# Around the attention stage of a two-layer model: where the low part of the inverse matrix is made, an early use of Gelu, the first block rows of the experts, and the place of the result rows

## The chip, the cores and the metric

One core of a Trainium2 chip runs the whole program in one launch. The metric is the device time in microseconds (us) of that core. TensorE multiplies (PE in the rows, its weight loads are PEld), VectorE is DVE, ScalarE is ACT, GpSimd is POOL, and SyncE (SP) only starts transfers. A queue of SP, ACT or POOL is written SPq, ACTq, POOLq.

## What is computed

Two layers on x of 8 x 512 x 256 (the batch b has 8 entries), all in float32. Cut to what matters here:

```python
xn = layernorm(x)
x = x + attention(xn) * silu(ffn(xn))          # layer 0: causal attention, 16 heads of 16
xn = layernorm(x)
# layer 1, s: a long convolution. v = short 3-tap filter of one branch of a projection,
# conv = irfft(rfft(v) * rfft(filter)), s = (branch * conv) @ out_w + out_b
# layer 1, g: mixture of 20 experts, 2 for each row
h = gelu(xn @ wg1 + bg1); probs = softmax(h @ wg2 + bg2); top 2 of 20
y[row] = sum over its 2 experts of prob * (xn[row] @ We[e] + be[e])
x = x + s * silu(y)
```

## The kernel before, in words

The program is three blocks of code (`with nc.Block()`), each with one instruction stream for each engine. A block ends when all five engines have come to its end; GpSimd's stream ends with a drain. The order of work within a stream is written out by hand, and semaphores join the streams.

**Block 1 (from L641).** For each b: attention and feed-forward of layer 0, the residual, the norm of layer 1 (`norm(b, NORM_X1)`, whose rows are made by L1365), the transposed normed rows `xn2T`, the router (hidden layer with Gelu L1195, logits, softmax with Exp L1199, top 2, ranks L616 to L629) and `send` (L637): eight indirect DMAs of GpSimd, which scatter the rows to `slots_in`, sorted by expert. The routing of b runs during the attention of b+1; for the last b, 7, it stands alone behind the attention. There the streams also prepare layer 1's convolution: the inverse transform's matrix `Inv` is split into a high part (ACT, L1320) and a low part (POOL, L1771, which reads the staging tile `st_i`), and the first projection, short filter and forward transform are run. GpSimd's stream there is: low part of `Win` (L1767), the power that gives 1/std of the norm (`power`, L1683), low part of `Inv` (L1771), a wait for the ranks, a tiny operation (L1774), eight sends. VectorE's is: norm of b = 7, `short_filter(0)`, `split_x1(7)`, router, ranks, `split_v_low(0)`, `block_tables()`. The last of these makes `block_row` and `block_expert` (L1633, L1634): for each of 84 blocks of 128 rows, where it starts in `slots_in` and which expert it has.

**Block 2 (from L1835), the expert stage.** 84 blocks, 6 in a ring (14 turns of 6). SP reads the block's row out of SBUF into a register (`value_load`, L1822) and starts the transfer of 128 rows (L1824) into one of 12 places of `xb`. TensorE transposes them (L1856), ACT copies (L1893), TensorE multiplies by the expert's matrix (L1871), DVE adds the bias (L1915), ACT stores three blocks at a time (L1901). TensorE waits for three blocks' transfers at a time (semaphore `xb_in`, one for each half of a ring). DVE also does the product with the filter of the convolution's entry b = 0 in seven parts (`with_filter`, first at the second turn) and writes it to `Z`, which lies over `st_win` and `st_i`. GpSimd has nothing in this block.

**Block 3 (from L1976), the last stage.** Turn b = 0 to 7. TensorE's turn is `pe_turn`: projection of b+1, `back_whole(b)` (the inverse transform's first half, needs the first split of `Z`), `transposes(b+1)` (L347), `back_mixed(b)` (L371), `forward(b+1)` (L302, waits for `v2_lo`, the low part of the filtered branch), `project_out(b)` (L383). ACT follows with copies out of PSUM; `transformed` (L417) gives `Vf`, the transform that DVE multiplies by the filter. DVE's turn for b = 1 to 6 is: `filtered(b)` (first instruction L469, which waits for two of the four `Vf`), `branch_out(b-1)`, `short_filter(b+1)` (L440), `split_z_low(b, 1)` (L453), `split_v_low(b+1)` (L447, waits for ACT's L409 and makes `v2_lo`), `gated(b)` (L526, waits for L371), `result_rows(b-1)` (L1969 and L1973: product with the gate, sum with the residual rows), `second_choice(b)` (L1961, four instructions). GpSimd gathers the experts' rows (L2050) for ACT's `first_choice` and DVE's `second_choice`.

Of the kernel before, what the change touches and what calls it, by code (L numbers as in the profile page):

```python
# [11 lines left out]
ALU = mybir.AluOpType  # L12
# [3 lines left out]
P = 128  # L16
# [17 lines left out]
NROWS = NE * CAP  # L34
# [20 lines left out]
def program(nc, x, wqkvT, woutT, wguT, wdT, wg1, bg1, wg2, bg2, winT, bin_, short, wo2, bo2, fw1, fb1, fw2, fb2,  # L55
# [15 lines left out]
    with ctx:  # L71
# [103 lines left out]
        rinv = keep("rinv", [P, NT, NH])  # L175
        idle_p = keep("idle_p", [P, NH])
        idle_v = keep("idle_v", [P, 2])
        Mneg = keep("Mneg", [P, 1, NT, GH])
        Mhi = keep("Mhi", [P, NT, GH], F32R)
        Mparts = keep("Mparts", [P, 2, GH, NT])  # L180
# [275 lines left out]
        def with_filter(dve, b, part):  # L456

            def step(ins):
                ins.then_inc(U["dstep"], 1)

            def done(n):
                dve.wait_ge(U["dstep"], ND * b + n)

            flat = lambda ap: ap.rearrange("p q c -> p (q c)")
            re = lambda h_: flat(Vf[:, h_, 0:2, :])
            im = lambda h_: flat(Vf[:, h_, 2:4, :])
            tb = lambda t_, h_: flat(t_[:, h_, :, :])
            def mul(at, a_, b_):
                step(dve.tensor_tensor(at, a_, b_, ALU.mult))  # L469

            t = [tmp[:, n, :] for n in range(4)]
            q = [tmq[:, n, :] for n in range(4)]
            if part == 0:
                dve.wait_ge(U["vf_sb"], 4 * b + 2)
                at_least(dve, U["z_lo"], 2 * b)
                mul(t[0], re(0), tb(HA, 0))
                mul(t[1], im(0), tb(HB, 0))
                mul(t[2], re(0), tb(HB, 0))
            if part == 1:
                mul(t[3], im(0), tb(HN, 0))  # L480
                done(2)
                step(dve.tensor_tensor(flat(Z[:, 0, 0:2, :]), t[0], t[1], ALU.subtract))
                done(4)
                step(dve.tensor_tensor(flat(Z[:, 0, 2:4, :]), t[2], t[3], ALU.add))
            if part == 2:
                mul(q[0], re(0), tb(HA, 1))
                mul(q[1], im(0), tb(HB, 1))
                mul(q[2], re(0), tb(HB, 1))
            if part == 3:
                mul(q[3], im(0), tb(HN, 1))  # L490
                dve.wait_ge(U["vf_sb"], 4 * b + 4)
                done(6)
                mul(t[0], re(1), tb(HA, 0))
                mul(t[1], im(1), tb(HB, 0))
            if part == 4:
                mul(t[2], re(1), tb(HB, 0))
                mul(t[3], im(1), tb(HN, 0))
                done(10)
                step(dve.tensor_tensor(q[0], q[0], q[1], ALU.subtract))
            if part == 5:  # L500
                step(dve.tensor_tensor(q[2], q[2], q[3], ALU.add))  # L501
                done(14)
                step(dve.tensor_tensor(t[0], t[0], t[1], ALU.subtract))  # L503
                step(dve.tensor_tensor(t[2], t[2], t[3], ALU.add))  # L504
            if part == 6:
                done(17)
                at_least(dve, U["s_ps"], 2 * b)
                step(dve.tensor_tensor(flat(Z[:, 1, 0:2, :]), q[0], t[0], ALU.add))
                done(18)
                step(dve.tensor_tensor(flat(Z[:, 1, 2:4, :]), q[2], t[2], ALU.add))  # L510
# [130 lines left out]
        with nc.Block() as block:  # L641
# [493 lines left out]
            def _(act):  # L1135
# [184 lines left out]
                act.activation(Inv[:, HI, :, :], st_i[:, :, :], ACT.Copy).then_inc(t_hi, 1)  # L1320
                projected(act, 0, (0, 1))
                first_tap(act, 0)
                split_x1(B - 1)
                projected(act, 0, (2,))
                route_hidden(B - 1)
# [354 lines left out]
            def _(pool):  # L1680
# [86 lines left out]
                pool.tensor_tensor(Win[:, LO, :, :], st_win[:, :, :], f(Win[:, HI, :, :]), ALU.subtract  # L1767
                                   ).then_inc(t_lo, 1)
                power(B - 1, veps2, rstd2, "ln2_var", "ln2_std")
                pool.wait_ge(t_hi, 3)  # L1770
                pool.tensor_tensor(Inv[:, LO, :, :], st_i[:, :, :], f(Inv[:, HI, :, :]), ALU.subtract)  # L1771
                pool.wait_ge(S["ranked"], B)
                pool.wait_ge(S["ln2_done"], NT * B)
                pool.tensor_tensor(idle_v[:, 1:2], neghalf[:, 0:1], neghalf[:, 0:1], ALU.mult)  # L1774
# [43 lines left out]

            return ap.rearrange("(j k p) d -> j p k d", p=P, k=HALF)[n]

        def load_block(sp, block, after=0):
            row = sp.value_load(block_row[0:1, block:block + 1], min_val=0, max_val=NROWS - P)  # L1822
            at_least(sp, transposed, after)
            sp.dma_start(xb[:, block % AHEAD, :], slots_in[bass.ds(row, P), :]  # L1824
                         ).then_inc(xb_in[block % AHEAD // HALF], 16)
# [9 lines left out]
        with nc.Block() as block:  # L1835
            @block.sync
            def _(sp):
                sp.wait_ge(S["sent"], 128 * B)
                for n in range(NBLK):
                    load_block(sp, n, after=n - AHEAD + 1)  # L1840
                    if n == AHEAD:
                        sp.dma_start(bo2b[:, :], bo2.partition_broadcast(P)).then_inc(U["wo_in"], 16)
                sp.wait_ge(U["wo_in"], 32)
# [44 lines left out]
            def _(act):  # L1888
# [12 lines left out]
                    act.dma_start(half_rows(slots_out, h_), yb[:, HALF * (h_ % 2):HALF * (h_ % 2) + HALF, :]  # L1901
                                  ).then_inc(yb_out[h_ % 2], 16)

                in_turns(act, lambda: None, turn)
                store(NBLK - 1)

            @block.vector
            def _(dve):
# [67 lines left out]
        with nc.Block() as block:  # L1976
# [39 lines left out]
            def _(dve):  # L2016
                for b in range(B):
# [6 lines left out]
                    if not last:  # L2024
                        short_filter(dve, b + 1)
                        split_z_low(dve, b, 1)
                        split_v_low(dve, b + 1)
                        gated(dve, b)
                    else:
                        split_z_low(dve, b, 1)  # L2030
                    if b > 0:
                        result_rows(dve, b - 1)
                    second_choice(dve, b)
                    if last:
# [75 lines left out]
```

## Time and profile before

| what | value |
| --- | --- |
| device time, median of 3 runs | 1112.41 us (1111.92 to 1112.5) |
| the profiled execution, device time | 1105.52 us |
| its span | 1103.8 us |
| busy share over the span: PE, DVE, ACT, POOL | 89%, 65%, 44%, 37% |

The page of the profile cuts the span into 40 equal slices of 27.6 us. Each digit is the busy share in tenths (9 is 90% or more); PEclk is the granted clock of TensorE in tenths.

```profile
PE   1889999999999999999999999966599989999995
PEld 1765776676686686686586676645366768888884
DVE  7556465576676666666667456546266338999997
ACT  2434544544635635534545543453122334444441
POOL 6203312522522532441441452263000044778860
PEclk9978997998998998998999996997899999999998
DMA  4863944542642733634534540087467743334421
```

Slices 1 to 26 are block 1; slices 27 to 29 hold the work behind the last attention, the change of blocks and the start of the expert stage; the expert stage ends in slice 33, and the last stage fills the rest. The share of a busy engine is a mean over stages: what a change is worth is read from the rows of its stage.

### The profile page before, as it was taken

The numbers are of one execution on the slowest core, as the hardware profiler recorded it, in microseconds if no ns is written. First come the engines' busy times: TensorE is split into PE (matmuls) and PEld (weight loads), VectorE is DVE, ScalarE is ACT, GpSimd is POOL, SyncE is SP. The second block draws the span as 40 slices with busy tenths as digits, with TensorE's granted clock in tenths as the row PEclk, the third lists the DMA queues.
The fourth block names the chain that finished last, engine by engine and source line by source line (L and its number), as shares of the span: only waits on it lengthen the run. The fifth ranks groups of instructions, "written<-read, shape, count | busy, mean of one in ns | idle before, by whom it ended". The sixth has DMA issues, their size and how long they took to land. (4 is left out here: it accounts for less than half of the span.)

```text
span 1103.8 us, 19164 instructions
## 1 busy us (share of the span) xinstructions
PE 978.5 (89%) x5936; PEld 746.5 (68%) x5936; DVE 717.7 (65%) x1459; ACT 480.2 (44%) x887; POOL 408.9 (37%) x610
## 2 busy tenths in 40 slices
PE   1889999999999999999999999966599989999995
PEld 1765776676686686686586676645366768888884
DVE  7556465576676666666667456546266338999997
ACT  2434544544635635534545543453122334444441
POOL 6203312522522532441441452263000044778860
PEclk9978997998998998998999996997899999999998
DMA  4863944542642733634534540087467743334421
GB/s 172 160 149 61 172 155 60 108 162 44 113 148 53 116 131 81 90 123 115 77 97 135 82 125 29 2 288 274 129 202 215 217 174 100 110 123 131 131 80 38
DMA packets 87596, 137.23 MB, mean 124 GB/s; under 512 B 9907, under 2 KB 63347, under 8 KB 85364
## 3 DMA queue, kind: packets, MB, share of 16 engines
q1 hardware_dynamic: 69188, 101.40, 37.5%
q0 software_dynamic: 6144, 16.79, 4.9%
q10 hardware_dynamic: 12208, 18.35, 4.7%
q8 instruction: 28, 0.46, 0.2%
q14 instruction: 28, 0.23, 0.1%
HBM read 79.88 MB, written 55.57 MB: 123 GB/s over the span
## 5 line engine op out<-in xcount | busy, mean ns | idle before, releaser
L1449 DVE TENSOR_REDUCE Mneg<-PS 128x2 f32<-128x1024 f32 (+2 forms) x192 | 195.6, 1043 | 103.8 <-PE PS L961 103.6
L1210 ACT ACTIVATE PT<-PS 128x512 f32<-128x512 f32 (+1 forms) x384 | 170.0, 537 | 165.6 <-PE PS L985 165.2
L1698 POOL TENSOR_TENSOR idle_p<-neghalf 128x1 f32<-128x1 f32 x128 | 25.1, 196 | 353.7 <-ACT PT L1210 353.7
L985 PE MATMUL PS<-qs,ks 96*128 96x512 f32 (+3 forms) x512 | 140.8, 388 | 12.2 <-ACT PT L1210 5.7
L957 PE MATMUL PS<-ks,qs 96*128 96x256 f32 (+3 forms) x512 | 132.8, 371 | 0.8 <-DVE Mneg L1449 0.8
L985 PEld LDWEIGHTS PS<-qs,ks 96*128 96x128 f32 x512 | 96.9, 210 | 42.1 <-ACT PT L1210 25.7
L785 PE MATMUL PS<-xnT,Wgu 128*128 128x512 f32 x384 | 104.5, 414 | 4.0 <-ACT V L1155 2.4
L1871 PE MATMUL PS<-Wes,xbT 128*128 x336 | 97.3, 397 | 3.8 <-issue 2.1
L1704 POOL TENSOR_SCALAR_AFFINE_SELECT PT<-PT 128x256 f32<-128x256 f32 x256 | 99.7, 413 | 0.0
L957 PEld LDWEIGHTS PS<-ks,qs 96*128 96x128 f32 x512 | 86.8, 218 | 11.1 <-issue 7.6
L785 PEld LDWEIGHTS PS<-xnT,Wgu 128*128 128x128 f32 x384 | 71.0, 194 | 23.5 <-DVE h L1392 2.9
L998 PE MATMUL PS<-PT,V 128*32 128x512 f32 (+3 forms) x1024 | 82.1, 464 | 4.1 <-POOL PT L1704 4.0
L1687 POOL TENSOR_TENSOR h<-h,h 128x512 fp32r<-128x512 f32 x40 | 51.3, 1288 | 65.7 <-ACT h L1174 65.6
L1915 DVE TENSOR_TENSOR yb<-PS,bes 128x256 f32<-128x256 f32 x84 | 35.2, 424 | 62.1 <-PE PS L1871 53.0
L2046 POOL TENSOR_TENSOR idle_q<-ident 128x1 f32<-128x1 f32 x8 | 66.6, 8319 | 23.6 <-DVE acc L1961 23.6
L2050 POOL DMA_INDIRECT yg<-slots_out,pos x64 | 66.7, 1043 | 18.6 <-issue 17.6
L961 PE MATMUL PS<-mask,ident 128*128 128x128 f16 (+2 forms) x352 | 69.6, 276 | 0.0
L1871 PEld LDWEIGHTS PS<-Wes,xbT 128*128 128x128 f32 x336 | 52.3, 191 | 24.5 <-issue 22.1
L637 POOL DMA_INDIRECT slots_in<-xn,rows_now x64 | 62.3, 974 | 17.5 <-issue 17.5
L1893 ACT ACTIVATE xbT<-PS 128x256 f32<-128x256 f32 x84 | 31.6, 384 | 85.1 <-PE PS L1856 64.2
L998 PEld LDWEIGHTS PS<-PT,V 128*32 128x32 f32 x1024 | 32.2, 116 | 51.0 <-issue 40.5
L1392 DVE SCALAR_TENSOR_TENSOR h<-PS,sil 128x512 f32<-128x512 f32 x48 | 32.5, 689 | 44.4 <-ACT sil L1167 31.7
(227 smaller groups left out, 1760.3 us busy)
## 6 DMA issues: line engine op xcount, KB each, us to landing
qs<-qk_parts SPq DMA_DIRECT2D x96, 128.0 KB
ks<-qk_parts SPq DMA_DIRECT2D x96, 128.0 KB
xb<-slots_in SPq DMA_DIRECT2D x84, 128.0 KB, 2.3
slots_out<-yb ACTq DMA_DIRECT2D x28, 384.0 KB, 3.2
qk_parts<-qhl SPq DMA_DIRECT2D x16, 512.0 KB, 3.1
qk_parts<-khl SPq DMA_DIRECT2D x16, 512.0 KB, 2.6
xn2T_parts<-xn2T SPq DMA_DIRECT2D x8, 1024.0 KB, 4.9
xT<-xn2T_parts ACTq DMA_DIRECT2D x7, 1024.0 KB, 4.9
```

The source lines that it names most:

```text
L637: pool.indirect_dma_start(slots_in, bass.IndirectOffsetOnAxis(rows_now[:, t, k:k + 1], axis=0), xn2[:, t, :], None).then_inc(S["sent"], 16)
L785: last = pe.matmul(out, lhs(i, c), rhs(j, c), start=last is None, stop=n == 0)
L957: pe.matmul(out, qs[:, hd, P * qt:P * qt + P], ks[:, hd, 0:keys], start=n % a_bank == 0, stop=False, skip_group_check=True)
L961: last = pe.matmul(diagonal[:, :, keys - P:keys], ident16[:, :], mask16[:, :].unsqueeze(1).to_broadcast([P, a_bank, P]), start=False, stop ...
L985: last = pe.matmul(PS[:, 4 + n, col:col + T - P * kt], ks[:, hd, P * kt:P * kt + P], qs[:, hd, P * kt:T], start=True, stop=True)
L998: last = pe.matmul(PS[32 * j:32 * j + 32, 7, P * kt:T], V[:, kt, GH * g + j, :], PT[:, g % 2, j, COL[kt]:COL[kt] + T - P * kt], start=kt = ...
L1210: act.activation(PT[:, g % 2, j, 512 * n:512 * n + width], PS[:, 4 + n, 0:width], ACT.Exp, scale=SCALE).then_inc(S["exped"], 1)
L1449: dve.tensor_reduce(out=Mneg[:, 0, qt, heads[0]:heads[-1] + 1], in_=all_of, op=ALU.max, axis=AX.X, negate=True).then_inc(S["maxed"], 1)
L1704: last = pool.affine_select(out=blocks, in_=blocks, compare_op=ALU.is_ge, fill=0.0, base=0, pattern=[[0, 2], [1, P]], channel_multiplier=-1)
L1871: ins = pe.matmul(PS[:, HALF + u % HALF, 0:C], xbT[:, u, c, :], Wes[:, bass.ds(expert, 1), c, :].rearrange("p o n -> p (o n)"), start=c == ...
L2046: pool.tensor_tensor(idle_q[:, 3:4], ramp_col[:, :], ramp_col[:, :], ALU.mult).then_inc(X["idle"], 1)
L2050: pool.indirect_dma_start(yg[:, n % 2, k, t, :], None, slots_out, bass.IndirectOffsetOnAxis(pos[:, n, t, k:k + 1], axis=0)).then_inc(X["go ...
```

## The change

Four edits behind the attention and in the last stage.

1. GpSimd's instruction that makes the low part of `Inv` (L1771) leaves block 1, with its wait for the high part. It is now the only instruction of GpSimd in block 2, followed by an increment of `t_lo`; DVE waits for `t_lo` = 3 ahead of the first filter part of b = 0, since `Z` overwrites `st_i`.
2. ACT runs one Gelu on one column of 128 elements, into a new tile `idle_a`, behind `first_tap(0)` and ahead of `split_x1(7)`, so before the router's own Gelu.
3. In block 2 SP reads the rows of blocks 0 and 2 into registers first, then waits for the sends, and starts blocks 0, 2, 3, 4 and on. The row of block 1 is read by ACT, which also starts that block's transfer on its own queue.
4. In the last stage, for b = 1 to 6, DVE does `result_rows(b-1)` between `split_z_low(b, 1)` and `split_v_low(b+1)`, and no longer behind `gated(b)`. For b = 0 there is none, and for b = 7 its place is as before.

```diff
--- before.py
+++ after.py
@@ -175,6 +175,7 @@
         rinv = keep("rinv", [P, NT, NH])
         idle_p = keep("idle_p", [P, NH])
         idle_v = keep("idle_v", [P, 2])
+        idle_a = keep("idle_a", [P, 1])
         Mneg = keep("Mneg", [P, 1, NT, GH])
         Mhi = keep("Mhi", [P, NT, GH], F32R)
         Mparts = keep("Mparts", [P, 2, GH, NT])
@@ -471,6 +472,8 @@
             t = [tmp[:, n, :] for n in range(4)]
             q = [tmq[:, n, :] for n in range(4)]
             if part == 0:
+                if b == 0:
+                    dve.wait_ge(t_lo, 3)
                 dve.wait_ge(U["vf_sb"], 4 * b + 2)
                 at_least(dve, U["z_lo"], 2 * b)
                 mul(t[0], re(0), tb(HA, 0))
@@ -1320,6 +1323,7 @@
                 act.activation(Inv[:, HI, :, :], st_i[:, :, :], ACT.Copy).then_inc(t_hi, 1)
                 projected(act, 0, (0, 1))
                 first_tap(act, 0)
+                act.activation(idle_a[:, :], neghalf[:, 0:1], ACT.Gelu)
                 split_x1(B - 1)
                 projected(act, 0, (2,))
                 route_hidden(B - 1)
@@ -1767,8 +1771,6 @@
                 pool.tensor_tensor(Win[:, LO, :, :], st_win[:, :, :], f(Win[:, HI, :, :]), ALU.subtract
                                    ).then_inc(t_lo, 1)
                 power(B - 1, veps2, rstd2, "ln2_var", "ln2_std")
-                pool.wait_ge(t_hi, 3)
-                pool.tensor_tensor(Inv[:, LO, :, :], st_i[:, :, :], f(Inv[:, HI, :, :]), ALU.subtract)
                 pool.wait_ge(S["ranked"], B)
                 pool.wait_ge(S["ln2_done"], NT * B)
                 pool.tensor_tensor(idle_v[:, 1:2], neghalf[:, 0:1], neghalf[:, 0:1], ALU.mult)
@@ -1818,8 +1820,10 @@
 
             return ap.rearrange("(j k p) d -> j p k d", p=P, k=HALF)[n]
 
-        def load_block(sp, block, after=0):
-            row = sp.value_load(block_row[0:1, block:block + 1], min_val=0, max_val=NROWS - P)
+        def row_of_block(eng, block):
+            return eng.value_load(block_row[0:1, block:block + 1], min_val=0, max_val=NROWS - P)
+
+        def load_block(sp, block, row, after=0):
             at_least(sp, transposed, after)
             sp.dma_start(xb[:, block % AHEAD, :], slots_in[bass.ds(row, P), :]
                          ).then_inc(xb_in[block % AHEAD // HALF], 16)
@@ -1835,9 +1839,13 @@
         with nc.Block() as block:
             @block.sync
             def _(sp):
+                first_rows = {n: row_of_block(sp, n) for n in (0, 2)}
                 sp.wait_ge(S["sent"], 128 * B)
                 for n in range(NBLK):
-                    load_block(sp, n, after=n - AHEAD + 1)
+                    if n == 1:
+                        continue
+                    row = first_rows[n] if n in first_rows else row_of_block(sp, n)
+                    load_block(sp, n, row, after=n - AHEAD + 1)
                     if n == AHEAD:
                         sp.dma_start(bo2b[:, :], bo2.partition_broadcast(P)).then_inc(U["wo_in"], 16)
                 sp.wait_ge(U["wo_in"], 32)
@@ -1901,8 +1909,18 @@
                     act.dma_start(half_rows(slots_out, h_), yb[:, HALF * (h_ % 2):HALF * (h_ % 2) + HALF, :]
                                   ).then_inc(yb_out[h_ % 2], 16)
 
-                in_turns(act, lambda: None, turn)
+                def before():
+                    row = row_of_block(act, 1)
+                    act.wait_ge(S["sent"], 128 * B)
+                    load_block(act, 1, row)
+
+                in_turns(act, before, turn)
                 store(NBLK - 1)
+
+            @block.gpsimd
+            def _(pool):
+                pool.tensor_tensor(Inv[:, LO, :, :], st_i[:, :, :], f(Inv[:, HI, :, :]), ALU.subtract
+                                   ).then_inc(t_lo, 1)
 
             @block.vector
             def _(dve):
@@ -2024,11 +2042,12 @@
                     if not last:
                         short_filter(dve, b + 1)
                         split_z_low(dve, b, 1)
+                        if b > 0:
+                            result_rows(dve, b - 1)
                         split_v_low(dve, b + 1)
                         gated(dve, b)
                     else:
                         split_z_low(dve, b, 1)
-                    if b > 0:
                         result_rows(dve, b - 1)
                     second_choice(dve, b)
                     if last:
```

## Rows read from the trace of the kernel before

**Rows 1.** Windows: us, then busy us (instructions) by engine, PEclk, DMA share, GB/s.
```profile
765.00:770.00 5.00, 5.00 (x32) 5.00 (x32) 3.54 (x20) 1.67 (x3) 3.78 (x5) 0.69 0.33 117
...
900.00:1090.00 190.00, 176.31 (x1037) 154.78 (x1036) 174.23 (x261) 86.33 (x130) 129.17 (x67) 0.99 0.34 109
```

**Rows 2.** Line L1365, all its instructions: duration min/median/max in ns.
```profile
L1365 DVE TENSOR_SCALAR xn<-xres,mv,rstd x32: 401/409/4592, 140.5 to 746.5; 128x256 f32<-128x256 f32 x32
```

**Rows 3.** Timeline behind the last attention: start us, us, engine, line [idle before, releaser].
```profile
741.29 4.48 POOL L1771 TENSOR_TENSOR Inv<-st_i,Inv 128x2048 fp32r<-128x2048 f32 x1
...
741.34 5.56 DVE L1365 TENSOR_SCALAR xn<-xres,mv,rstd 128x256 f32<-128x256 f32 x4 [1.15 <-POOL rstd L1683]
...
746.95 1.97 PE L879 MATMUL PS<-ident,xn 128*128 128x128 f32 x8 [8.15 <-DVE xn L1365]
...
748.96 1.02 ACT L1191 ACTIVATE xn2T<-PS 128x1024 fp32r<-128x1024 f32 x1 [8.02 <-PE PS L879]
...
751.29 1.66 PE L785 MATMUL PS<-xn2T,Wg 128*128 128x512 f32 x6
...
752.06 1.28 ACT L1195 ACT_TABLE_LOAD   x1
...
753.36 0.69 ACT L1195 ACTIVATE hgT<-PS,bg1c 128x512 f32<-128x512 f32 x1
...
756.02 0.27 ACT L1199 ACTIVATE lge<-lg 128x80 f32<-128x80 f32 x1 [0.68 <-DVE lg L1409]
...
761.23 0.19 POOL L1774 TENSOR_TENSOR idle_v<-neghalf 128x1 f32<-128x1 f32 x1 [15.45 <-DVE row_in L629]
```

**Rows 4.** Timeline at the end of block 1.
```profile
770.51 0.96 POOL L637 DMA_INDIRECT slots_in<-xn,rows_now  x1 [0.30 <-issue]
...
771.54 0.24 DVE L1634 CAST block_row<-PS 128x84 int32<-128x84 f32 x1
```

**Rows 5.** GpSimd's drain at the end of block 1: duration ns, start us.
```profile
L641 POOLq DRAIN  x1: 15569/15569/15569, 761.2 to 761.2; - x1
```

**Rows 6.** SP's reads of block rows at the start of block 2: min/median/max ns.
```profile
L1822 SPq TENSOR_LOAD <-block_row x7: 267/268/485, 777.0 to 783.9; - x7
```

**Rows 7.** Timeline of block 2: SP's transfers, first transposes, DVE's first filter part.
```profile
778.04 0.36 SPq L1824 DMA_DIRECT2D xb<-slots_in  x1
...
780.28 0.33 SPq L1824 DMA_DIRECT2D xb<-slots_in  x1
...
782.30 1.54 PE L1856 MATMUL PS<-ident,xb 128*128 128x128 f32 x6 [10.97 <-DMA xb<-slots_in]
...
795.15 0.68 DVE L469 TENSOR_TENSOR tmp<-Vf,HA 128x512 f32<-128x512 f32 x1
```

**Rows 8.** Timeline of one turn of the last stage, and the next turn's first instruction.
```profile
941.51 0.68 DVE L469 TENSOR_TENSOR tmp<-Vf,HA 128x512 f32<-128x512 f32 x1
...
958.52 1.23 DVE L453 TENSOR_TENSOR Zs<-Z,Zs 128x1024 fp32r<-128x1024 f32 x1
...
958.67 1.09 PE L347 MATMUL PS<-ident,cv 128*128 128x128 f32 x8 [1.63 <-DVE cv L440]
...
959.80 1.03 ACT L409 ACTIVATE v<-PS 128x1024 fp32r<-128x1024 f32 x1 [3.36 <-PE PS L347]
...
960.86 1.23 DVE L447 TENSOR_TENSOR v<-PS,v 128x1024 fp32r<-128x1024 f32 x1 [1.11 <-ACT v L409]
...
962.77 3.50 PE L302 MATMUL PS<-v,Fwd 128*128 128x256 f32 x28
...
963.58 1.22 DVE L1969 TENSOR_TENSOR acc<-sg,s 128x1024 f32<-128x1024 f32 x1
...
965.83 0.60 ACT L417 ACTIVATE Vf<-PS 128x512 f32<-128x512 f32 x1 [0.84 <-PE PS L302]
...
965.97 0.48 DVE L1961 SCALAR_TENSOR_TENSOR acc<-yg,gates,acc 128x256 f32<-128x256 f32 x1
...
967.55 0.69 DVE L469 TENSOR_TENSOR tmp<-Vf,HA 128x512 f32<-128x512 f32 x1
```

## The prediction, written before the changed kernel was seen

> **What bounds the kernel now.** I read the slices of the page first, to find where TensorE is not full: slices 27 to 29, behind the last attention, and the last stage, where TensorE and VectorE are both near full. The edits lie in these two places. The order of reading is then: the timeline behind the attention, the drain that ends block 1, SP's first transfers of block 2, and one turn of the last stage.
>
> Behind the attention the work is one chain, with every engine waiting for the one before. DVE's four row norms L1365 take 5.56 us [rows 3], though an instruction of that line and form takes 0.409 at the median of 32 and only one took 4.592 [rows 2]. That one starts 0.05 us behind GpSimd's 4.48 us pass L1771, and the four end (746.9) some 1.1 us after the pass (745.77), which is three normal ones: the first did nothing until the pass was over [rows 3]. TensorE's transposes L879 had by then waited 8.15 us for the norm, ACT's copy L1191 8.02. From there the chain is: L879, L1191, router's hidden layer L785, its Gelu at 753.36, logits, softmax, ranks, GpSimd's L1774 at 761.23, eight sends, the last from 770.51 to 771.47 [rows 3, 4]. Block 1 doesn't end there: GpSimd's drain was reached at 761.2 and lasted 15.569 us, to 776.8, so 5.3 us past the last send [rows 4, 5]. The block tables were ready at 771.78 [rows 4], 5 us early, so the tables do not set the end. SP's first read of a row stands at 777.0 [rows 6], directly behind the drain. So each us taken out of the chain ahead of L1774 is a us of the span.
>
> Block 2 then starts with SP alone: a transfer at 778.04, the third at 780.28, and the first transposes at 782.30, since TensorE waits for three blocks; it had been idle 10.97 us [rows 7]. Two full periods between starts, 2.24 us, show 1.12 us for each block on SP, of which the transfer instruction is 0.33 to 0.36 and the rest is the read of the row (0.27) and register work [rows 6, 7].
>
> In the last stage a turn takes 26.04 us, from 941.51 to 967.55 [rows 8]. Over 190 us, DVE is busy 174.2 and TensorE 176.3, at a granted clock of 0.99 [rows 1]. Neither is alone the bound: they hand the turn to each other. DVE waits 1.11 us ahead of L447, TensorE 1.63 ahead of L347 [rows 8].
>
> **Edit 1, the low part of the inverse matrix.** Removed from the path: 4.59 - 0.41 = 4.18 us. I take all of it. L440, behind the norm on DVE, moves up too. TensorE does the transposes and six matmuls of the projection ahead of L785; they have the same lengths and move with it. The cost of the pass in block 2 is nothing: GpSimd starts it at about 777.2 and needs 4.48, so to 781.8, when DVE has no work, and DVE's new wait comes only at its first filter part, at 795.15 [rows 3, 7]. Queued behind that wait are DVE's bias adds, then ACT and TensorE; there are 13 us of cover, and if the pass took longer than that, each us more would be paid. Bounds for the edit: 3.5 us, if some other arrival (a transfer under load) holds L785 half a us later, to 4.2.
>
> **Edit 2, Gelu early.** Without a load ahead of it, the router's Gelu can start when L785 is done: 751.29 + 1.66 = 752.95, against 753.36 [rows 3]. With a few hundredths for the handover this gives 0.37 us. The load (1.28) and the one-column Gelu move into ACT's wait ahead of L1191: 8.02 us now and 3.8 after edit 1, which still covers some 1.5. Without that cover the load would hold L1191, and so the router. The next load, Exp's, is covered: ACT had it done 0.68 us before the logits came, and uses 0.37 of that now [rows 3]. Bounds 0 to 0.4.
>
> The trace shows a load as 1.28 us with the Gelu 0.01 behind its end [rows 3]. The Trainium skill, ScalarE: Activation LUTs, What ACT_TABLE_LOAD costs, puts a switch at 2.66 us, 1.28 of load and 1.38 of drain. By that page the exposed part would be about 1.4 us more and the edit worth some 1.75; the row decides, and it shows no drain.
>
> **The two together** are 4.55 us ahead of L1774. Sends and drain follow at their own pace. What could be late next is the transfers: the sends would now start at 756.7 and end at 766.9, over more of the last large loads. The DMA share is down to 0.33 in 765 to 770 [rows 1], so the last sends meet a quiet queue even then, and the drain keeps its 5.3 us.
>
> **Edit 3, first block rows.** SP reads two rows (1.0 us for the first up to its transfer, now one read and its register work, some 0.6, later), then starts blocks 0 and 2 with about 0.5 us between: block 0 at 778.6, block 2 at 779.2. ACT's read and transfer of block 1 take as long as SP's first, 778.1. The third transfer starts at 779.2 instead of 780.28: 1.1 us, and blocks 3 and on follow 1.1 earlier as well, so the stage keeps it: everything in it starts from the barrier. Bounds: 0.3 (transfers of two queues delay each other, or the stage's later hiccups come elsewhere) to 1.9.
>
> **Edit 4, result rows.** Work is the same; only waits change. In the row's times: L453 ends at 959.75. L1969 and L1973 need 2.39 us (963.58 to 965.97) and would now run from 959.7 to 962.1; their inputs, the gate of the entry before and its branch, are a turn old. This swallows DVE's 1.11 us wait, but L447 starts at 962.1 instead of 960.86, 1.2 later, and ends at 963.3. TensorE, which went on to `forward` at 962.77 without a wait, now has to wait until 963.35, 0.6 later. The second `Vf` follows 3.66 us behind (965.83 + 0.60 = 966.43 before), so at 967.0. DVE, meanwhile: two L526 with no wait, four L1961, free at 966.0, and waits for `Vf`. L469 starts at 967.05 instead of 967.55: 0.5 us a turn. TensorE's wait ahead of L347 shrinks to 1.63 - 0.5 - 0.6, some 0.5, still above nothing, so it doesn't take over [rows 8]. Six turns, b = 1 to 6: 3.0 us. Lower bound 0, if handovers cost a little more than the rows show; upper bound 1.11 a turn, 6.7, if `Vf` did not hold DVE.
>
> **Sum.** 4.18 + 0.37 + 1.1 + 3.0 = 8.65. Span 1103.8 to 1095.2, device time of the profiled execution 1105.5 to 1096.9. The median of the runs shown, 1112.41, lies 6.9 above it; I subtract the same 8.65 there: 1103.8.
>
> **Rivals.**
> - *The result rows bring nothing*: the delay of `v2_lo` costs TensorE what DVE wins. For it: both engines are within 2 us of the turn's length; against it: 1.1 us of DVE's slack to `Vf` in the turn of before. 1112.4 - 5.65 = 1106.8. Chance 0.13.
> - *They bring the whole wait*, 1.11 a turn, because TensorE catches up: 12.3 in all, 1100.1. Against it: `forward` has no slack in the rows. 0.05.
> - *The chain behind the attention is not what is late*: the long L1365 has another cause, or transfers behind the sends hold the drain. Then about 4.1 us remain of edits 3 and 4: 1108.3. Against it: the one in 32, and its end with the pass [rows 2, 3]. 0.07.
> - *No change to speak of*: that and the result rows' failure together, 1.1 left: 1111.3. 0.03.
> - *Slower*: TensorE now has two waits in each turn (ahead of L347 and of `forward`), and its granted clock falls from 2.4 to 1.2 GHz in each of six turns. Each us of work at the lower level costs one more; it decides from 8.65 / 6 = 1.45 us a turn. With 3 us in each it would be 18 - 8.65, so 1121.8. Against it: with one wait of 1.63 us in each turn the clock stays at 0.99 [rows 1, 8], and the two new ones are shorter, about 0.6 each. 0.02.
>
> **How the numbers follow.** The forecast has 0.70, the rivals 0.13, 0.05, 0.07, 0.03, 0.02. Bounds of the terms around the sum: gain 5.2 to 11.4. I put the range from 1101.0 to 1107.2: it takes in the forecast and the first rival and leaves out the others, 0.17. Faster by over 0.2% (2.2 us, about what a measurement of this kernel can tell from no change): 0.95; within it 0.03; slower 0.02.
>
> **What would show it.** In the profile of the changed kernel: the four L1365 of the last norm 1.6 us in sum; no load between L785 and the router's Gelu, one behind the first tap; GpSimd's drain to its end 4.5 us earlier; GpSimd's pass in the first 5 us of block 2 and no wait of DVE on it; three first transfers, one from ACT, within 1.1 us, first transposes 4.4 us behind the drain, 5.5 before; turns of 25.5 us with DVE waiting for `Vf` and not ahead of L447. It is wrong if the pass still finds a DVE instruction to block, if the drain's end doesn't move with the sends, or if turns stay at 26.0.

## The result, and the profile after

The changed kernel takes 1098.36 us (median of 4 runs, 1093.73 to 1100.0), the kernel before beside it 1112.45 (1111.92 to 1114.03): ratio 0.9864, 95% interval 0.9832 to 0.9896. That is 14 to 15 us less, where 8.65 were forecast. The time lies 2.6 us under the range's low end. Executions that lie over 1.5% above the fastest one of their kernel are left out of all comparisons here.

The profiled execution of the changed kernel has a span of 1098.3 us and a device time of 1100.0, the slowest of its four; the profiled one of before had 1103.8 and 1105.5, which is faster than all four that were timed. So the two traces are only 5.5 us apart, at the same mean granted clock of 0.935, and the two traces alone can't show 14 us.

First the stretch behind the attention. The timeline of the changed kernel (start us, us, engine, line, operation [idle before, releaser]); it answers to [rows 3, 4, 7]:

```profile
741.60 1.28 ACT L1326 ACT_TABLE_LOAD   x1
742.09 1.38 DVE L1369 TENSOR_SCALAR xn<-xres,mv,rstd 128x256 f32<-128x256 f32 x4 [1.16 <-POOL rstd L1687]
742.89 0.20 ACT L1326 ACTIVATE idle_a<-neghalf 128x1 f32<-128x1 f32 x1
...
743.53 1.97 PE L882 MATMUL PS<-ident,xn 128*128 128x128 f32 x8 [4.08 <-DVE xn L1369]
...
747.87 1.84 PE L788 MATMUL PS<-xn2T,Wg 128*128 128x512 f32 x6
...
749.75 0.69 ACT L1198 ACTIVATE hgT<-PS,bg1c 128x512 f32<-128x512 f32 x1 [0.97 <-PE PS L788]
...
757.62 0.19 POOL L1776 TENSOR_TENSOR idle_v<-neghalf 128x1 f32<-128x1 f32 x1 [15.56 <-DVE row_in L632]
...
766.90 0.96 POOL L640 DMA_INDIRECT slots_in<-xn,rows_now  x1 [0.30 <-issue]
773.44 4.49 POOL L1922 TENSOR_TENSOR Inv<-st_i,Inv 128x2048 fp32r<-128x2048 f32 x1 [5.58 <-POOLq L644]
774.37 0.36 ACTq L1828 DMA_DIRECT2D xb<-slots_in  x1
775.01 8.50 SPq L1828 DMA_DIRECT2D xb<-slots_in  x9
777.68 1.54 PE L1864 MATMUL PS<-ident,xb 128*128 128x128 f32 x6 [11.05 <-DMA xb<-slots_in]
```

The four norms take 1.38 us instead of 5.56, TensorE waits 4.08 for them instead of 8.15, the table load stands behind the first tap, and the router's Gelu has none ahead of it. GpSimd's pass L1922 is over at 777.9, 12.5 us before VectorE's first filter part, at 790.44.

Then the last stage. L348 (L347 before) is TensorE's identity product of the short filter, once a turn; the distance from one start to the next is the turn. The changed kernel, same columns:

```profile
903.15 1.03 PE L348 MATMUL PS<-ident,cv 128*128 128x128 f32 x8
928.70 1.09 PE L348 MATMUL PS<-ident,cv 128*128 128x128 f32 x8 [1.49 <-DVE cv L441]
954.62 1.09 PE L348 MATMUL PS<-ident,cv 128*128 128x128 f32 x8 [0.83 <-DVE cv L441]
980.53 1.09 PE L348 MATMUL PS<-ident,cv 128*128 128x128 f32 x8 [0.82 <-DVE cv L441]
...
1058.27 1.09 PE L348 MATMUL PS<-ident,cv 128*128 128x128 f32 x8 [0.81 <-DVE cv L441]
```

The kernel before:

```profile
907.04 1.03 PE L347 MATMUL PS<-ident,cv 128*128 128x128 f32 x8
932.61 1.09 PE L347 MATMUL PS<-ident,cv 128*128 128x128 f32 x8 [1.51 <-DVE cv L440]
...
1062.90 1.09 PE L347 MATMUL PS<-ident,cv 128*128 128x128 f32 x8 [1.63 <-DVE cv L440]
```

Turns are 25.91 us where they were 26.06. Counted from the start of the four norms (741.34 before, 742.09 after), which leaves the attention out:

| point | before | after | less |
|---|---|---|---|
| GpSimd's idle_v ahead of the sends | 19.89 | 15.53 | 4.36 |
| first transposes of block 2 | 40.96 | 35.59 | 5.37 |
| first L347 / L348 | 165.70 | 161.06 | 4.64 |
| last L347 / L348 | 321.56 | 316.18 | 5.38 |
| end | 362.46 | 356.21 | 6.25 |

In this pair of traces the expert stage gives 0.73 us back. TensorE's clock rises from 1.2 to 2.4 GHz only some time after the transposes begin. Windows of three us from the first transposes (us, busy us by engine, PEclk, DMA share, GB/s), before:

```profile
782.30:785.30 3.00, 3.00 (x10) 2.19 (x10) 0.00 (x0) 1.15 (x3) 0.00 (x0) 0.53 0.44 131
785.30:788.30 3.00, 2.88 (x16) 2.09 (x16) 0.85 (x2) 0.77 (x2) 0.00 (x0) 1.00 0.38 118
```

and after, where the second three are at 0.71, so part of them is still at 1.2 GHz:

```profile
777.70:780.70 3.00, 3.00 (x10) 2.17 (x10) 0.00 (x0) 1.15 (x3) 0.23 (x1) 0.50 0.40 116
780.70:783.70 3.00, 2.50 (x11) 1.95 (x11) 0.74 (x2) 0.59 (x2) 0.00 (x0) 0.71 0.48 139
```

Two questions remained: why edit 4 brings 0.15 us a turn and not 0.5, and why the timed runs differ by 14 us where the traces show six.

### The profile page after: what moved, and what is told of

Same layout as the page of the kernel before. It is cut to its first block and busy times, and to the rows that moved or that the text cites. A ratio compares the mean times of both kernels' runs of the same rounds, so it can differ in the third digit from the quotient of the medians.

```text
span 1098.3 us, 19168 instructions
## 1 busy us (share of the span) xinstructions
PE 981.7 (89%) x5936; PEld 747.7 (68%) x5936; DVE 714.3 (65%) x1459; ACT 479.9 (44%) x888; POOL 341.9 (31%) x610
## 5 line engine op out<-in xcount | busy, mean ns | idle before, releaser
L988 PE MATMUL PS<-qs,ks 96*128 96x512 f32 (+3 forms) x512 | 141.0, 389 | 11.5 <-ACT PT L1213 5.8
L788 PE MATMUL PS<-xnT,Wgu 128*128 128x512 f32 x384 | 105.4, 417 | 4.0 <-ACT V L1158 2.4
L960 PEld LDWEIGHTS PS<-ks,qs 96*128 96x128 f32 x512 | 86.6, 217 | 11.1 <-issue 7.6
L788 PEld LDWEIGHTS PS<-xnT,Wgu 128*128 128x128 f32 x384 | 71.5, 195 | 23.8 <-DVE h L1396 3.1
L303 PE MATMUL PS<-v,Fwd 128*128 128x256 f32 x432 | 56.1, 289 | 5.3 <-issue 2.8
```

Source lines behind the costliest of these rows:

```text
L303: last = pe.matmul(PS[:, bank + 2 * half + part, C * (q_ % 2):C * (q_ % 2) + C], Fwd[:, i, kc, P * q_:P * q_ + P], src[:, j, 2 * half + kc ...
L788: last = pe.matmul(out, lhs(i, c), rhs(j, c), start=last is None, stop=n == 0)
L960: pe.matmul(out, qs[:, hd, P * qt:P * qt + P], ks[:, hd, 0:keys], start=n % a_bank == 0, stop=False, skip_group_check=True)
L988: last = pe.matmul(PS[:, 4 + n, col:col + T - P * kt], ks[:, hd, P * kt:P * kt + P], qs[:, hd, P * kt:T], start=True, stop=True)
```

## The experiments

No kernel below leaves work out. Times and clocks are compared within a job, that is, with the kernel before run beside. In the job of the first four the kernel before took 1139.4 us, at a mean granted clock of 0.915; in the three later jobs it took 1110.5 to 1112.5, at 0.929 to 0.932. The first and the second job ran on the same chip, so why the first was slower isn't known. Some 9 of its 27 us lie in the first turn of the last stage: it takes 33.9 to 34.9 us in all four traces of that job, with and without edit 4, and 25.4 to 25.6 in the later ones. TensorE waits 5.7 to 7.8 us in it, and the turn's mean clock is 0.90. The texts use letters: Theory A says that what is measured beyond the stages' 6 us is the clock's chance; its rival B, that it belongs to the edits, at equal clock. C puts edit 4's lost gain on GpSimd's gathers. D concerns the pass that blocks VectorE. E and F say where a change of clock comes from.

**One edit at a time.** All four edits, the same code as the changed kernel:

> The changed kernel once more, beside the kernel before on the same chip. Theory A (the edits bring what the stages of the two traces show, counted from SP's first transfer behind the attention: 4.2 for the path ahead of the sends, 1.1 for the block rows, about 1.1 for the result rows, 0.7 given back in the expert stage; the rest of the 14 us measured is the attention stage's granted clock, which no edit touches): 5.5 to 7 us less than before once the time up to that transfer is the same, and spans that differ by more than that only where the mean granted clock differs. Theory B (the edits themselves bring the 14 us, in a place the two traces don't show): ratio 0.987 again, with equal granted clock in both kernels.

Measured: 1129.56 us, ratio 0.9931 (0.9888 to 0.9974); mean clock 0.918 against 0.915.

Edit 1 alone:

```
-                pool.wait_ge(t_hi, 3)
-                pool.tensor_tensor(Inv[:, LO, :, :], st_i[:, :, :], f(Inv[:, HI, :, :]), ALU.subtract)
...
+            @block.gpsimd
+            def _(pool):
+                pool.tensor_tensor(Inv[:, LO, :, :], st_i[:, :, :], f(Inv[:, HI, :, :]), ALU.subtract
+                                   ).then_inc(t_lo, 1)
```

> Edit 1 alone. Theory A: 4.2 us less than before (ratio 0.9962), L1774's counterpart 4.2 us earlier counted from SP's first transfer behind the attention. Theory B: about 11 us less, since the other three bring 3 at most.

Measured: ratio 0.9954 (0.9915 to 0.9994), norms of 1.38 us. The interval holds edit 1's 4.18 us (0.9963).

Edit 4 alone:

```
                         split_z_low(dve, b, 1)
+                        if b > 0:
+                            result_rows(dve, b - 1)
                         split_v_low(dve, b + 1)
```

> Edit 4 alone. Theory A as the trace of after has it: turns of 25.93 us instead of 26.05, the gathers of GpSimd moved into DVE's filter part and its instructions 0.05 us longer there; 1.1 us less than before in all, ratio 0.999. Rival (the prediction's): turns of 25.5, 3.0 us less.

Measured: ratio 0.9969 (0.9927 to 1.001), turns of 25.91 us.

Edits 2 and 3 alone (idle_a's Gelu; rows 0 and 2 read ahead, block 1 from ACT):

> Edits 2 and 3 alone. Theory A: Gelu without a load 0.3 to 0.4 us, first transposes 1.1 us earlier behind the barrier, 1.5 us less in all if the expert stage keeps them, 0.8 if it gives 0.7 back as in the trace of after. Theory B: 1.5 or more.

Measured: 1.0019 (0.9982 to 1.0056). Its first transposes stood 4.7 us behind the barrier (5.5 before), so edit 3 does what it says; its gain can't be seen in the time, and the interval still holds the 0.8 to 1.5 us expected. In this job the intervals are as wide as the effects; it settles little more than that all four are faster together.

**Is 14 us chance?** The same code as before, as a null test:

> The kernel before against itself, for what two medians of the same code differ by. Theory A (most of the 14 us beyond the stages' sum is the granted clock of the moment): ratio within 0.996 to 1.004 but single executions 10 us and more apart, longer by about 10.8 us for each 0.01 of mean granted clock less. Rival (the comparison is steady to 0.2%, so the 14 us belong to the change): executions within 0.2%.

Measured: ratio 1.0001 (0.9976 to 1.0025), single executions from 1107.1 to 1119.0 us.

The changed kernel again, beside it:

> The changed kernel beside e5 and e6 on their chip. Theory A: ratio 0.992 to 0.996 and 5 to 6 us less at equal granted clock. Theory B (14 us): 0.987.

Measured: 1101.39 us, ratio 0.9884 (0.9854 to 0.9915), clock 0.937 against 0.929. 11.1 us less by the medians. The interval lies below the 0.992 to 0.996 of Theory A, so the surplus is not the chance of one comparison. But Theory B wanted it at equal clock, and it comes with a higher clock again: what recurs is that the changed kernel runs at a higher mean clock.

**Where edit 4's gain went.** GpSimd's rows in one turn. In the changed kernel:

```profile
936.17 0.19 POOL L2065 TENSOR_TENSOR idle_q<-ident 128x1 f32<-128x1 f32 x1 [13.56 <-DVE acc L1979]
936.50 0.98 POOL L2069 DMA_INDIRECT yg<-slots_out,pos  x1
...
945.77 0.95 POOL L2069 DMA_INDIRECT yg<-slots_out,pos  x1 [0.30 <-issue]
```

In the kernel before:

```profile
941.67 13.15 POOL L2046 TENSOR_TENSOR idle_q<-ident 128x1 f32<-128x1 f32 x1 [15.14 <-DVE acc L1961]
954.96 0.98 POOL L2050 DMA_INDIRECT yg<-slots_out,pos  x1
```

A one-column product took 13.15 us before: it started 0.16 us into VectorE's filter part and was held until it was over. Now VectorE has a free 1.08 us ahead of its filter part, the product passes in it in 0.19 us, and the eight gathers that follow run beside the filter part. VectorE in the changed kernel:

```profile
937.16 0.69 DVE L470 TENSOR_TENSOR tmp<-Vf,HA 128x512 f32<-128x512 f32 x1 [1.08 <-ACT Vf L418]
...
939.68 0.68 DVE L485 TENSOR_TENSOR Z<-tmp 128x512 f32<-128x512 f32 x1
940.28 0.73 DVE L487 TENSOR_TENSOR Z<-tmp 128x512 f32<-128x512 f32 x1
940.93 0.68 DVE L470 TENSOR_TENSOR tmq<-Vf,HA 128x512 f32<-128x512 f32 x1
...
954.48 1.22 DVE L454 TENSOR_TENSOR Zs<-Z,Zs 128x1024 fp32r<-128x1024 f32 x1
...
958.01 1.22 DVE L448 TENSOR_TENSOR v<-PS,v 128x1024 fp32r<-128x1024 f32 x1
```

The step from L487 to the next is 0.65 us where others are 0.60. From the filter's start to the second L454 there are 17.32 us; before, 17.01 [rows 8]. The test holds the gathers until the filter part is over:

```
+                    if n >= 2:
+                        pool.wait_ge(U["dstep"], ND * n)
```

> The changed kernel with GpSimd's gathers of the last stage held until DVE's filter part of the turn is over, where they ran in the kernel before. Theory C (the gathers, now early, lengthen DVE's L469 instructions from 0.60 to 0.65 us from start to start, and that eats the result rows' gain): DVE's filter part shrinks from 17.3 back to 17.0 us, turns from 25.92 to 25.6, 2 us less in all than the changed kernel. Rival (TensorE or ACT sets the rest): turns stay at 25.9.

Measured: ratio 0.9844 (0.9804 to 0.9884). Its VectorE:

```profile
942.45 0.69 DVE L470 TENSOR_TENSOR tmp<-Vf,HA 128x512 f32<-128x512 f32 x1 [1.08 <-ACT Vf L418]
...
959.47 1.23 DVE L454 TENSOR_TENSOR Zs<-Z,Zs 128x1024 fp32r<-128x1024 f32 x1
...
968.08 0.69 DVE L470 TENSOR_TENSOR tmp<-Vf,HA 128x512 f32<-128x512 f32 x1 [1.08 <-ACT Vf L418]
```

17.02 us from filter to L454, and a turn of 25.63. Theory C is shown: the gathers beside the filter part cost 0.3 us a turn. Whether it is GpSimd's instructions or the transfers that they start was not separated.

**Could the pass stay where it was, in pieces?**

```
-                pool.tensor_tensor(Inv[:, LO, :, :], st_i[:, :, :], f(Inv[:, HI, :, :]), ALU.subtract)
+                for q_ in range(NQ):
+                    pool.tensor_tensor(Inv[:, LO, q_, :], st_i[:, q_, :], f(Inv[:, HI, q_, :]), ALU.subtract)
```

> The kernel before with GpSimd's pass over the inverse matrix cut into four instructions of 512 columns, in the same place (about 1.1 to 1.2 us each). Theory D (a DVE norm instruction waits for the one GpSimd instruction it meets): the first waits 1.2 us, and the four need 2.5 to 3 us, if none of the rest is caught again; L1774 1.5 to 3 us earlier than before. Rival (each of the four norm instructions meets one GpSimd instruction, or DVE is held while GpSimd has any queued): the four need 5 us and more, L1774 as before.

Measured: ratio 0.9976 (0.9953 to 0.9999). The norms in the groups of instructions of 745 to 751 us (busy us, mean ns | idle time before them):

```profile
L1365 DVE TENSOR_SCALAR xn<-xres,mv,rstd 128x256 f32<-128x256 f32 x4 | 5.2, 1351 | 1.2 <-POOL rstd L1683 1.2
```

The four take 5.17 us at 1351 ns each: now every one waits for a piece of the pass, where one had waited for the whole. Theory D falls, its rival holds: a norm gets through only between two of GpSimd's instructions, and four pieces take 0.39 us off the norms where taking the pass away takes 4.18. The Trainium skill (SBUF — State Buffer, SBUF: two separate sides) says that the port pair which the two engines share is locked for a whole instruction and not divided by bandwidth; both traces agree, with 4.59 us for the one norm under the whole pass [rows 2] and 1.351 for each under a quarter.

**Which edits carry the surplus?** Edits 1 to 3 without edit 4, edit 4 alone, all four, and the gathers held, on one chip:

> Edits 1 to 3 together, the result rows left in the old order. Theory E (what the clock gives back comes from the last stage's order of turns: the old order lets the granted clock fall inside a turn, 6 falls in 30 turns of five traces, the new order none in 30): this kernel keeps those falls, its mean clock stays near that of the kernel before, and it gains what its stages show, 4 to 6 us, ratio 0.995. Theory F (the clock comes from the shorter stretch between the attention and the first block): this kernel has most of it, 9 to 12 us, ratio 0.990. In its profile six turns of 26.05 us, or 27.5 where a fall is, by E and F alike.

Measured: ratio 0.9932 (0.9897 to 0.9968), mean clock 0.9339 against 0.9305.

> Edit 4 alone, on this chip. Theory E: its stages give about 1 us and the higher clock the rest, 6 to 10 us, ratio 0.992 to 0.995, with a mean clock 0.004 or more above that of the kernel before. Theory F: 1 to 2 us, ratio 0.999, with the clock of the kernel before. Turns of 25.9 us with no fall inside one by both.

Measured: 0.9995 (0.9971 to 1.0019), clock 0.9303.

> The changed kernel's code, beside the others for comparison on one chip. All theories: ratio 0.984 to 0.990 (11 to 16 us less), stage turns 25.9 us. If e9 and e10 add up to it, the edits act singly; if the two sum to less, the clock needs both.

Measured: 0.9894 (0.9849 to 0.9938), clock 0.9370.

> The changed kernel with GpSimd's gathers held until VectorE's filter part has ended. Turns 25.63 us instead of 25.91, so six turns give 1.7 us over the changed kernel at equal clock: ratio 0.0015 below that of the changed kernel beside it, with an interval that will hardly part the two. If the 0.0040 between the two in the earlier job was the effect and not the clock's spread, the same gap returns.

Measured: 0.9871 (0.9831 to 0.9912), turns of 25.63. The order of the two is that of the first pair, by 0.0023.

Edits 1 to 3 carry most of it, 7 us; edit 4's own value is 0.6 us, not distinguishable from none. Theory E as written, that edit 4 alone brings the higher clock, has failed (0.9303). For edits 1 to 3 the measured ratio lies between E's 0.995 and F's 0.990, and its interval holds both. E's falls inside turns are real all the same. The kernel before has turns of 27.56 us in some executions. From its trace in the null test:

```profile
961.73 1.09 PE L347 MATMUL PS<-ident,cv 128*128 128x128 f32 x8 [1.63 <-DVE cv L440]
962.87 4.63 PE L371 MATMUL PS<-Inv,Zs 128*128 128x256 f32 x24
...
989.29 1.09 PE L347 MATMUL PS<-ident,cv 128*128 128x128 f32 x8 [1.63 <-DVE cv L440]
```

L371 takes 3.1 us in a turn of 26.05. The window over the start of this turn shows why, the second one shows the clock back at 2.4 GHz:

```profile
961.70:966.70 5.00, 4.93 (x27) 4.69 (x28) 3.03 (x3) 2.61 (x5) 3.78 (x5) 0.66 0.46 157
966.70:971.70 5.00, 5.00 (x44) 5.00 (x43) 4.13 (x6) 1.20 (x2) 1.63 (x2) 1.00 0.29 86
```

TensorE had waited 1.63 us just ahead of it. Count the turns from the second L347 or L348 on, six in a trace. In seven traces with the old order 8 of 42 have such a fall: all three that begin with a wait of 2.0 to 2.1 us, 5 of the 32 with one of 1.61 to 1.64, and none of the seven with 1.3 to 1.5. A turn with a fall is 1.3 to 1.5 us longer. In nine traces with the new order none of 54 has one: the wait is 0.54 to 0.84 in 45 of them and 1.3 to 1.5 in nine. Not counted are the long first turn of the first job and the end of the last turn, where the clock falls in every kernel.

**Is it the length of the wait?** The changed kernel with two instructions of the short filter made twice:

```
+                    if k == 1:
+                        dve.scalar_tensor_tensor(out=cv[:, 2 - k, m, :], in0=vt[:, m, k:k + T],
+                                                 scalar=shortc[:, m, k:k + 1],
+                                                 in1=cv[:, k - 1, m, :], op0=ALU.mult, op1=ALU.add
+                                                 ).then_inc(U["twice"], 1)
+                        dve.wait_ge(U["twice"], 2 * b + m + 1)
```

> The changed kernel with VectorE's first two short-filter instructions of each turn made twice, so that TensorE's wait ahead of L348 (0.83 us in the changed kernel, 1.63 in the kernel before) grows to about 2.2. Theory E (the longer wait in the old order's turn is what lets the granted clock fall inside a turn): falls come back, in about one turn of five or more, each a turn 1.5 us longer; the mean clock goes back to 0.933 or below, and the kernel is 1.4 x 7 = 10 us of work plus 2 us or more of falls above the changed kernel, 1113 us or more, ratio 1.000. Rival (the falls have to do with what is issued where, not with the length of this wait): no falls, clock as in the changed kernel, 1111 us or less, ratio 0.998 or less; turns of 27.3 us.

> The same kernel once more, for a second trace of seven turns and twelve more times: falls inside turns in this trace or the one before by Theory E, in neither by its rival; the mean clock of both together within 0.002 of 0.930 by Theory E, of 0.936 by the rival.

Measured: 1.0025 (0.9996 to 1.0053) and 1.0019 (0.999 to 1.0047), clock 0.933 in both, and 0.932 for the kernel before beside them. L348 in the second:

```profile
934.76 1.97 PE L348 MATMUL PS<-ident,cv 128*128 128x128 f32 x8 [3.06 <-DVE cv L447]
963.91 1.34 PE L348 MATMUL PS<-ident,cv 128*128 128x128 f32 x8 [2.35 <-DVE cv L447]
991.98 1.97 PE L348 MATMUL PS<-ident,cv 128*128 128x128 f32 x8 [2.34 <-DVE cv L447]
1019.97 1.10 PE L348 MATMUL PS<-ident,cv 128*128 128x128 f32 x8 [2.33 <-DVE cv L447]
```

The falls are back, in three turns of each trace. In the second L348 itself shows them (1.97 and 1.34 us instead of 1.09); in the first they are seen in L372 behind it, which takes 4.63, 4.23 and 3.77 us instead of 3.12. The turns with one take 28.25, 28.01 and 27.87 us in the first and 29.15, 28.07 and 27.99 in the second, so 0.4 to 1.7 more than the 27.48 of the turns without. So in the new order too, a wait of 2.3 us can let the clock fall, though it did in six turns of twelve only, and one of 0.8 was never seen to. The clock of both together, 0.933, lies between the ranges that Theory E and its rival gave. In the same job edits 1 to 3 and all four edits have 0.937 and 0.938: with the longer wait most of that lead is gone.

**Is the gap between the sum and the parts real?**

> Edits 1 to 3 without the result rows once more. If edits 1 to 3 give 5.3 us by their stages and the rest is edit 4 and its clock, this stays at ratio 0.993 to 0.995, and falls inside turns are seen again in about two of six turns. If the 4.6 us between this kernel and the changed one in the earlier job was chance, it comes out at 0.990 or below.

Measured: 0.9937 (0.9901 to 0.9973). No fall in this trace.

> The changed kernel's code beside the three others. Ratio 0.986 to 0.990 if the earlier three comparisons hold; no fall inside a turn (none in eight traces of the new order so far). If e15 and the result rows' own 0.9995 multiply to this ratio within 0.002, the edits act singly; if it is lower by more, something is left that only their sum brings.

Measured: 0.9901 (0.9864 to 0.9937). The parts multiply to 0.9937 x 0.9995 = 0.9932; the whole is 0.0031 lower, over the 0.002 set beforehand, but inside the intervals, each of which is 0.0036 wide to either side. It is not settled whether only the sum brings something. Edit 4 alone ought to have won its turns (1 us by the traces) and the falls (about 1.7 us a run, see below). It measured 0.6 us, with 2.7 us of uncertainty to either side, which neither shows nor excludes that.

## Why the prediction was right or wrong

Pooled over the three later jobs (means): before 1111.5 us in 87 runs, all four edits 1100.3 in 21, edits 1 to 3 1102.8 in 21, edit 4 alone 1110.8 in 12, gathers held 1097.8 in 11. One slope for all their times and clocks, with a level for each kernel, gives 9.3 us less for each 0.01 of mean granted clock, with a scatter of 1.4 us. At the equal clock of 0.93 it gives: before 1112.2, edits 1 to 3 1107.7, edit 4 1111.0, all four 1107.0, gathers held 1105.1; each difference is known to about 0.8 to 1.0. So the edits save 5.2 us at an equal clock, and 5.9 us more go with a clock of 0.9372 instead of 0.9308 (0.0064 x 925). Of the 0.0064, edits 1 to 3 bring 0.0046.

This split is not one of causes. Taking out time in which TensorE waits at 1.2 GHz raises the mean clock without making anything faster. In the trace of before the granted clock is 0.50 in the wait for the norms, 741.3 to 747.0, and so it is after, 742.1 to 743.5. 4.3 us at 0.50, taken out of a run at 0.931, raise its mean by 0.0017, which the slope would price at 1.5 us. So by this estimate some 1.5 of the 5.9 us can be the edits' own, counted as clock.

*Edit 1, 4.18.* Right to the hundredth: 5.56 less 1.38. The cover in block 2 held as well, and VectorE never waited for it.

*Edit 2, 0.37.* From L788's start to the Gelu it is 1.88 us, before 2.07 [rows 3]: 0.19, since L788 itself took 1.84 instead of 1.66. The load moved with its 1.28 us: it starts at 741.60, 0.02 us behind the end of the instruction ahead of it, and the Gelu starts 0.01 us behind the load. The Trainium skill (ScalarE: Activation LUTs, What ACT_TABLE_LOAD costs) gives 1.38 us of drain with a load; the trace of after shows none on either side, as that of before.

*The two together, 4.55.* 4.36 at the sends. The drain's end moved with them, 5.3 us behind the last send as before.

*Edit 3, 1.1.* 1.01 at the first transposes, as worked out: they stand 4.5 to 4.7 us behind the drain in eight traces with the edit, 5.5 to 5.6 in four without. "The stage keeps it" was the failing clause. From the first transposes to the first L347 or L348 the shortest are 124.7 us without the edit and 125.2 with it, so some 0.5 to 0.7 is given back. In the pair shown the clock rose later behind the first transposes. But the same distance goes up to 128.5 and 129.1 in other traces, and against that spread no gain of this edit can be seen in the times.

*Edit 4, 3.0.* This step failed. The half of the turn that was worked out behaved: from the second L454 to the next filter part 8.61 us instead of 9.03, with VectorE waiting for Vf. The other half was called unchanged ("Work is the same; only waits change"), and it grew by 0.31, because the gap that VectorE now has lets GpSimd's product pass and the gathers move into the filter part. With them held the turn is 25.63, the 0.4 us that was left of the forecast 0.5. In the pair of traces edit 4 is worth 0.74 us between first and last L348. Behind the last L348 there are another 0.87 less, but there the clock falls at different places in the two, so they are not to be put down to the edit.

*The sum and its level.* This step failed too, and it is what took the time out of the range. The sum of the stages was subtracted from the median as if the mean clock would stay as it was. Two errors stood against each other: the traces' 6.25 us are 2.4 less than the 8.65 forecast and would have given 1106.2, inside the range; the median went past its low end because the changed kernel also has a higher mean clock. That the clock could move in favour was in no term and no rival. The range was narrower than its own terms, too: their bounds add up to a gain of 3.8 to 13.2 us, the range allowed 5.2 to 11.4. And part of the miss is the luck of four runs: in the three later comparisons all four edits measured 1101.4, 1100.4 and 1101.7 us, at the range's low end, 9 to 11.5 less than the kernel before beside them.

The one rival on the clock took it to fall from the new waits. It did not: the two new waits are 0.8 and 0.4 us long, and in this place no wait under 1.6 us was seen to let it fall. [rows 8]'s 1.63 us was long enough in 5 of 32 turns, which one trace with a clock of 0.99 didn't show.

Where the 5.9 us that go with the clock come from is only partly shown. The stretch between attention and expert stage is at 0.81 in two traces of the kernel before and at 0.82 to 0.85 in four of the changed one, and 5 to 6 us shorter. (It is 0.84 in the trace with the pass in four pieces, where hardly anything was shortened, so the level alone proves little.) Its rows, before, and all four edits in the last job (columns as above):

```profile
721.20:794.30 73.10, 43.83 (x247) 34.56 (x246) 33.40 (x114) 23.80 (x38) 25.34 (x29) 0.81 0.71 244
```

```profile
714.20:781.70 67.50, 43.51 (x249) 34.80 (x248) 29.20 (x114) 23.95 (x39) 25.34 (x29) 0.85 0.77 265
```

The falls inside turns add about 8/42 x 6 x 1.5 = 1.7 us a run. From the start of the last norms to the end, the two traces of the kernel before have 362.5 and 369.4 us, the four of the changed one on these chips 356.2, 356.8, 359.7 and 356.7: on average 8.6 less, where 11.2 are timed. The missing 3 us or so aren't located: the two traced executions of before are themselves 3.1 us faster than the mean of its runs. Ahead of the norms, where the code is the same, one kernel's traces differ by 12 us (norms start at 734.2 in one, 746.4 in another). Traces of single executions can't tell chance from effect there, so this part stays open.

The version with the gathers held is the fastest of all, 0.9844 and 0.9871; its lead over the changed kernel, 1.9 us at equal clock, is shown by the turns (6 x 0.28 = 1.7) and not by the times alone.

## What to carry to other kernels

When an instruction is moved, read all engines through the whole period, not only the half in which it was and the half in which it goes: a new gap lets through whatever was held up behind the engine. Sum stages for the mechanism, but don't take one profiled execution for the median when TensorE's clock moves: here 0.01 of mean clock is worth more than any single edit. A wait of TensorE in a loop may cost more than its length, since the clock may fall behind it in some turns and not in others: look for that in several traces, not in one. And when two kernels are compared at equal mean clock, mind that the mean rises by itself where waiting at 1.2 GHz is taken out.

## What the runs showed of the hardware

- A GpSimd pass between SBUF tensors and VectorE's norms exclude each other, instruction by instruction: one pass of 4.48 us cost VectorE 4.18 us, four pieces of it 3.8 (5.17 less 1.38).
- The reverse holds too: a one-column product on GpSimd took 13.15 us beside VectorE's filter part and 0.19 in a gap ahead of it.
- Indirect gathers issued by GpSimd beside VectorE's two-operand instructions cost 0.31 us over 17 us.
- TensorE's granted clock fell to 1.2 GHz behind all 3 waits of 2.0 to 2.1 us at one place of a loop, behind 5 of 32 of 1.61 to 1.64, 6 of 12 of 2.3 to 3.1, none of 16 of 1.3 to 1.5, and none of 45 of 0.54 to 0.84.
- Two runs of one kernel differ by 9 us for each 0.01 of mean granted clock, and that mean goes from 0.927 to 0.940 for the kernel before in one job.
- A load of ScalarE's tables took 1.28 us, with 0.02 us ahead of it and 0.01 behind.
